# A graph-attention layer and a 64-expert layer in one kernel: the residual of a tile taken one step later, router work inside a tile's products, fewer routing operations on VectorE

## What is computed

```python
xn = layernorm(x);  h = xn @ W.T + b_W
e = (h @ a1)[:, None] + (h @ a2)[None, :] + b_a;  e = where(e > 0, e, 0.2 * e)
x = x + softmax(where(adj > 0, e, -9e15), axis=1) @ h
xf = layernorm(x)
logits = xf @ Wr + br;  topk_logits, topk_idx = top_k(logits, 2);  gates = softmax(topk_logits)
for e in range(64):
    out += combine[:, e:e+1] * (relu(xf @ W1[e] + b1[e]) @ W2[e] + b2[e])
x = x + out
```

## Time and profile before

| what | us |
|---|---|
| median of three runs | 293.51 |
| profiled execution | 295.59 |
| its span, first to last instruction | 293.8 |
| up to the first `scores` | 22.8 |
| attention loop with routing, to the last `place` | 147.2 |
| block tables, padding, first gather | 12.5 |
| 96 expert pairs | 94.5 |
| biases, sums, output | 16.8 |

### The profile page before, as it was taken

The page is one execution under the profiler, slowest core; times in us unless marked ns, Lnnn a source line. Parts: engine busy times, 40 slices in busy tenths (PEclk is TensorE's granted clock), DMA queues, the critical chain, the costliest instruction groups (busy, mean ns, idle before and its releaser), DMA issues.

```text
span 293.8 us, 6191 instructions
## 1 busy us (share of the span) xinstructions
PE 229.1 (78%) x1849; PEld 219.6 (75%) x1849; DVE 220.0 (75%) x643; ACT 173.5 (59%) x386; POOL 167.5 (57%) x193
## 2 busy tenths in 40 slices
PE   1491698596959779586997463999999999999840
PEld 1271698596959769585996352999999999999840
DVE  4858959949599986999997550588888666666554
ACT  2754665755765496567653602688786777777410
POOL 5840104325175982978886565344688888876500
PEclk9998599988897979899799655799999999999995
DMA  6992730644847386150298012212226830100057
GB/s 165 223 190 48 101 62 1 122 130 134 224 74 186 120 214 182 45 232 31 64 425 331 32 48 59 72 58 74 66 81 220 275 138 31 38 27 31 26 186 254
DMA packets 11120, 36.88 MB, mean 126 GB/s; under 512 B 2257, under 2 KB 2833, under 8 KB 10321
## 3 DMA queue, kind: packets, MB, share of 16 engines
q0 software_dynamic: 5232, 14.98, 22.5%
q1 hardware_dynamic: 5424, 21.11, 21.1%
q10 hardware_dynamic: 432, 0.40, 0.6%
HBM read 39.36 MB, written 5.51 MB: 153 GB/s over the span
## 4 chain that ended last, share of the span: by engine, by line
PE 44%; DVE 28%; POOL 9%; DMA 7%; issue 6%; ACT 4%; SPq 1%; POOLq 0%; DVEq 0%; ACTq 0%
PE bank L1089 16%; PE bank L1101 15%; DVE arena L697 7%; PE bank L986 6%; DVE arena L691 6%; POOL rstd L403 3%; POOL table L420 3%; POOL nm L405 2%; DMA arena<-result 2%; DMA xs<-in_x 2%; DVE arena L682 2%; DVE xs L703 1%; PE bank L938 1%; PE bank L1078 1%; ACT rows_in L546 1%
## 5 line engine op out<-in xcount | busy, mean ns | idle before, releaser
L986 PE MATMUL bank<-arena 128*128 128x130 f32 x512 | 64.8, 287 | 3.0 <-ACT arena L540 3.0
L986 PEld LDWEIGHTS bank<-arena 128*128 128x128 f32 x512 | 63.5, 204 | 3.9 <-issue 3.9
L1089 PE MATMUL bank<-arena 128*128 x384 | 61.1, 284 | 0.1
L1101 PE MATMUL bank<-w2s,arena 128*128 x384 | 59.2, 277 | 0.2 <-issue 0.2
L972 PE MATMUL bank<-ident,arena 128*128 128x128 f32 x256 | 39.0, 317 | 22.4 <-DVE arena L697 22.3
L420 POOL DMA_INDIRECT table<-rows_in,pos x32 | 46.8, 1464 | 15.9 <-issue 7.8
L972 PEld LDWEIGHTS bank<-ident,arena 128*128 128x128 f32 x256 | 34.9, 165 | 24.0 <-DVE arena L697 24.0
L1089 PEld LDWEIGHTS bank<-arena 128*128 128x128 f32 x384 | 52.1, 197 | 0.6 <-issue 0.3
L1101 PEld LDWEIGHTS bank<-w2s,arena 128*128 128x128 f32 x384 | 51.1, 194 | 0.6 <-issue 0.6
L868 DVE SCALAR_TENSOR_TENSOR arena<-bank,arena 128x128 f32 x96 | 33.6, 350 | 22.5 <-PE bank L1101 15.2
L599 ACT ACTIVATE arena<-bank,arena 128x128 f32<-128x128 f32 x96 | 35.2, 366 | 19.3 <-PE bank L1089 14.4
(11 more groups left out here) (191 smaller groups left out, 270.9 us busy)
## 6 DMA issues: line engine op xcount, KB each, us to landing
arena<-in_adj POOLq DMA_DIRECT2D x16, 512.0 KB, 6.5
w2s<-in_w SPq DMA_DIRECT2D x8, 768.0 KB
arena<-in_w SPq DMA_DIRECT2D x6, 1024.0 KB
arena<-in_w SPq DMA_DIRECT2D x4, 512.0 KB
w2s<-in_w SPq DMA_DIRECT2D x4, 512.0 KB
xs<-in_x SPq DMA_DIRECT2D x4, 256.0 KB, 6.4
arena<-result SPq DMA_DIRECT2D x2, 512.0 KB, 4.3
arena<-result SPq DMA_DIRECT2D x4, 256.0 KB, 6.2
```

The costliest lines, as they stand in the source:

```text
L986: ins = pe.matmul(OB[t % 2][:, 0:D + 2], pt_r[:, t % 2, j, :], h[:, j, :], start=(j == 0), stop=(j == T - 1))
L1089: ins = pe.matmul(hp(p, b), w1u[:, p % UW, P * b:P * b + P], xT_all[:, bass.ds(column, P)], start=True, stop=True)
L1101: ins = pe.matmul(yp(p), hT[:, p % UH, b, :], w2s[:, bass.ds(u, 1), b, :].rearrange("p e d -> p (e d)"), start=(b == 0), stop=(b == HB - 1))
```

## The change

Four things are altered:

1. **Residual.** VectorE's residual of tile s-3, not s-2, stands in step s, and it stands ahead of leaky(s-1). The statistics of a pair are therefore complete in an even step. GpSimd's `rstd_of` moves to even steps, behind the load of adj; ScalarE's norm(s-4), norm(s-3) stand ahead of evac(s-1) and no longer behind it. The pair 12, 13 is finished behind the loop. Tile 8 is written to the table in step 15, not 14.
2. **Router.** `route_a` and `route_b` of TensorE stand inside attend(LAST + 2): the transposes ahead of its first product, the logits behind the eighth. ScalarE's copy stands between the second and third bank of the same tile's evac.
3. **Fewer operations.** `hot` and `rk` are one operation each over both choices, in place of two. `posf` goes: the position is written as an integer at once. The row numbers (`ids`) are written into `rows_out` once, by GpSimd at the start, and not in each `place`.
4. **Biases.** The last stage's groups are four of four tiles, in place of six.

```diff
     COUNTED = 2
-    INLOOP = 4
-    PLACED = [(0, 0, 8), (0, 1, 9), (0, 2, 10), (0, 3, 11), (1, 4, 12), (1, 5, 13), (1, 6, 13), (1, 7, 14), (2, 8, 14), (2, 9, 15)]
+    PLACED = [(0, 0, 8), (0, 1, 9), (0, 2, 10), (0, 3, 11), (1, 4, 12), (1, 5, 13), (1, 6, 13), (1, 7, 14), (2, 8, 15), (2, 9, 15)]
...
+            pool.tensor_copy(rows_out[:, :, :, ID_COL], ids[:, :, :])
             pool.memset(cnt[:, 0, :], 0.0).then_inc(s_pool, 1)
...
             for s in range(T):
-                if s >= 3 and s % 2 == 1:
-                    rstd_of(s // 2 - 1)
                 if s + 5 < T:
                     load(s + 5)
+                if s >= 4 and s % 2 == 0:
+                    rstd_of(s // 2 - 2)
...
+            rstd_of(6)
             rstd_of(7)
...
             def evac(t):
                 for b in range(4):
+                    for q in range(NG):
+                        if b == 2 and t == LAST[q] + 2:
+                            route_a(q)
...
-                for q in range(INLOOP):
-                    if s == LAST[q] + 3:
-                        route_a(q)
+                if s >= 4 and s % 2 == 0:
+                    norm(s - 4)
+                    norm(s - 3)
                 if s >= 1:
                     evac(s - 1)
-                if s >= 3 and s % 2 == 1:
-                    norm(s - 3)
-                    norm(s - 2)
...
+            norm(T - 4)
+            norm(T - 3)
             evac(T - 1)
             norm(T - 2)
-            route_a(4)
             route_b(4)
...
-                for k in range(TOPK):
-                    ins = dve.tensor_tensor(hot[:, k, kept(q), :],
-                                            iota_e[:, :].rearrange("p (g e) -> p g e", g=1).to_broadcast([P, n, E]),
-                                            idxf[:, rows, k:k + 1].to_broadcast([P, n, E]), ALU.is_equal)
-                link(ins)
+                link(dve.tensor_tensor(hot[:, :, kept(q), :],
+                                       iota_e[:, :].rearrange("p (k g e) -> p k g e", k=1, g=1).to_broadcast([P, TOPK, n, E]),
+                                       idxf[:, rows, :].rearrange("p g (k e) -> p k g e", e=1).to_broadcast([P, TOPK, n, E]), ALU.is_equal))
...
-                link(dve.scalar_tensor_tensor(posf[:, :, 0:n], idxf[:, rows, :].rearrange("p g k -> p k g"), float(STRIDE),
-                                              rank[:, :, 0:n], ALU.mult, ALU.add))
                 dve.wait_ge(s_gate, q + 1)
-                dve.tensor_copy(rows_out[:, rows, :, ID_COL], ids[:, rows, :])
                 dve.tensor_copy(rows_out[:, rows, :, GATE_COL], gate[:, :, rows].rearrange("p k g -> p g k"))
-                dve.tensor_copy(pos[:, rows, :].rearrange("p g k -> p k g"), posf[:, :, 0:n]).then_inc(s_pos, 1)
+                dve.scalar_tensor_tensor(pos[:, rows, :].rearrange("p g k -> p k g"), idxf[:, rows, :].rearrange("p g k -> p k g"), float(STRIDE),
+                                         rank[:, :, 0:n], ALU.mult, ALU.add).then_inc(s_pos, 1)
...
                 if s + 1 < T:
                     penalty(s + 1)
+                if s >= 3:
+                    residual(s - 3)
                 leaky(s - 1)
-                if s >= 2:
-                    residual(s - 2)
...
+            residual(T - 3)
             leaky(T - 1)
             residual(T - 2)
...
             def attend(t):
...
-                if t == T - 1:
-                    route_a(4)
+                for q in range(NG):
+                    if t == LAST[q] + 2:
+                        route_a(q)
                 for j in range(T):
-                    if t == T - 1 and j == T // 2:
-                        route_b(4)
+                    for q in range(NG):
+                        if j == T // 2 and t == LAST[q] + 2:
+                            route_b(q)
```

More of the change, by code:

```diff
@@ L172, in build @@
         rank = sb("rank", [P, TOPK, GRP])
-        posf = sb("posf", [P, TOPK, GRP])
         pos = sb("pos", [P, T, TOPK], I32)
@@ L451, in _ @@
             rstd_of(8)
-            for q in (4, 5):
+            for q in range(4, NG):
                 for t in range(START[q], START[q + 1]):
@@ L622, in _ @@
                     fetch(p + UW - 1)
-            for q in range(NG):
+            for q in range(4):
                 act.wait_ge(s_ct, q + 1)
-                act.activation(combT[:, START[q] * P:START[q + 1] * P], bank[q][:, 0:SIZE[q] * P], ACT.Copy).then_inc(s_cts, 1)
+                act.activation(combT[:, q * 512:q * 512 + 512], bank[q][:, :], ACT.Copy).then_inc(s_cts, 1)
         @block.vector
@@ L899, in _ @@
             dve.tensor_scalar(y_all[:, NB - 1, :], y_all[:, NB - 1, :], slot_gate[:, NB - 1:NB], None, ALU.mult).then_inc(e_last, 1)
-            for q in range(NG):
+            for q in range(4):
                 base(q)
-            dve.wait_ge(s_base, NG)
+            dve.wait_ge(s_base, 4)
             for c in range(2):
@@ L1027, in _ @@
                 attend(s)
-                for q in range(INLOOP):
-                    if s == LAST[q] + 1:
-                        route_a(q)
-                    if s == LAST[q] + 2:
-                        route_b(q)
+                for q in range(NG):
                     if s == LAST[q] + 3:
```

27 lines of the change are left out of this document (13 added, 14 removed).

## The result

The changed kernel takes **281.13 us** (median of 4 runs, 280.18 to 282.84), where the kernel before takes 293.49 (293.38 to 293.85). The ratio is 0.958 with a 95% interval of 0.953 to 0.964: 12.4 us less. The forecast was 8.6 us less, 284.9, with a range from 282.0 to 288.8.

What follows compares the result with a forecast made beforehand. VectorE's list was taken to bound the loop, its waits being what could be gained. The terms -12.3 + 3.8 + 2.1 - 2.2 = -8.6 us from 293.5 gave 284.9 us; eight-in-ten range 282.0 to 288.8.

Steps and rivals of the forecast that it cites:

- The residual wait, -12.3: VectorE's waits at residual's first instruction in the loop: 13.2 us was to become 0.9, so -12.3 us.
- The chain of 11.9 us: From a pair's statistics to the products for residual(3): 14.9 us was to become 11.9, against VectorE's 11.4; wait left 0.5.
- Routing in the loop, +3.8: VectorE's new waits at top2 for logits: 0.7 us each for groups 0 and 1, 2.4 for group 2, 0 for group 3.
- It is 12.9. VectorE has ... 10.5: 2.4 us: Group 2: chain from statistics to logits 12.9 us, with rstd_of queued behind counts(1); VectorE has 10.5 us of work, wait 2.4.
- The end of the loop, +2.1: Group 4's logits: rstd_of 3.5 us late behind six table writes, wait 3.4 us where 1.3 was; bounds 0 and +6.5.
- Fewer operations, -2.2: VectorE's routing operations: 0.37 us saved in each of six groups, -2.2 us; bounds -2.8 and 0.
- the sign of being wrong in the clock: TensorE in the loop: running its odd products in 3.75 us everywhere would show the forecast wrong about the clock.
- A: Rival: all waits go, no new ones come, GpSimd's pair slips in, writes short: 278.1 us, between case near 282; chance 0.10.
- B: Rival: routing waits take more, through lower clock at two more groups and slow writes: 289 to 290 us; with D 0.14.
- C: Rival: slower, evac of the odd tile behind the norms, its wait reaching VectorE whole at seven places: 304 us; chance 0.04.
- D: Rival: GpSimd's table writes set the end, half of the gain goes: 289 us; chance 0.14 together with B.
- The rule weighed: Skill's inference that leaky leaves descriptor writes alone, so a table write costs 1.0 us; forecast kept the longer 2.48 us.

Runs made afterwards that it cites:

- Experiment 4's third kernel: Changed kernel with tile 9's table writes behind rstd_of(6), top2(3) behind the last leaky, and top2(0), top2(1) one step later: 281.46 us, ratio 0.959.
- experiment 4's first kernel: Changed kernel with the table writes of tile 9 moved behind rstd_of(6) on GpSimd's list: 281.13 us, ratio 0.954.
- experiment 1: Changed kernel with the old routing operations: 283.73 us, ratio 0.966; kernel before with only the fewer operations: 291.23 us, ratio 0.989.
- experiment 2: Changed kernel with residual(s-2) behind leaky(s-1): 298.6 us, ratio 1.016; with rstd_of also back in odd steps: 286.56 us, ratio 0.972.
- the third set: Kernels run on one chip beside the kernel before (293.46 us); the changed kernel, run again unaltered, took 280.13 us there, ratio 0.957.
- experiment 5: Changed kernel with six bias groups: 281.84 us, ratio 0.959; with twelve idle transposes behind products of tiles 6, 10, 12: 279.89 us, ratio 0.956.

## Why the prediction was wrong

Its direction and its mechanism held: the residual wait went, the logits' waits came in its place, and the operations gave a little. Terms of its sum were mis-sized, and most of them in one direction.

*The residual wait, -12.3: right, the last tenths by chance.* It measured 0.9 us where 0.9 was forecast, by 0.61 for the first tile (0.4) and none at residual(3) (0.5), and 0.27 at a place that the count had not named. The chain of 11.9 us measured 10.1, nearly all of the difference because it kept products of 5.5 us, which took 3.82.

*Routing in the loop, +3.8: the step that failed.* "The wait is 0.7, for groups 0 and 1 each" measured 0.79 and 0.79. "It is 12.9. VectorE has ... 10.5: 2.4 us" for group 2 measured 0: 2.4 us of the miss. The chain there took 8.2 us to the end of the logits. Of its 12.9, "3.9 us late" measured 3.1, the "3.1, near the middle" of GpSimd's pair 1.0, norms and hand-over 1.0 for 1.2, and the "1.7 for products at the lower clock" nothing. On GpSimd:

```profile
104.49 2.28 POOL L411 TENSOR_TENSOR cnt_t<-cnt,both 128x64 bf16<-128x64 bf16 x1 [3.48 <-DVE both L735]
106.85 1.01 POOL L411 TENSOR_TENSOR cnt_t<-cnt_t,both 128x64 bf16<-128x64 bf16 x2
107.94 0.31 POOL L413 TENSOR_TENSOR cnt<-cnt_t,both 128x64 bf16<-128x64 bf16 x1
108.40 0.99 POOL L419 DMA_INDIRECT table<-rows_in,pos  x1 [0.15 <-issue]
109.69 2.07 POOL L419 DMA_INDIRECT table<-rows_in,pos  x1 [0.30 <-issue]
111.78 0.73 POOL L402 TENSOR_TENSOR rstd<-ve,expo 128x2 f32<-128x2 f32 x1
112.59 0.19 POOL L404 TENSOR_TENSOR nm<-nm,rstd 128x2 f32<-128x2 f32 x1
```

The statistics were ready at 108.67, so `rstd_of` was 3.1 us late and not 3.9: the two counting operations at 106.85 take 1.01 us, where they took 2.94 before under a leaky. The write that leaky held ends 0.8 us behind leaky (begun at 108.59, 2.34 us long), and the pair of operations behind it falls into VectorE's small instructions of place(1), the first and last of which are:

```profile
110.85 0.16 DVE L742 TENSOR_SCALAR gs<-ge 128x4 f32<-128x4 f32 x1
...
112.85 0.16 DVE L753 SCALAR_TENSOR_TENSOR pos<-idxf,rank 128x8 int32<-128x8 f32 x1
```

"It starts at no fixed place of VectorE's step" was the error: the forecast itself had place(1), 1.9 us without a wide operation, on VectorE's list right behind leaky. The last 1.7 us, the lower clock, was not paid either (TensorE):

```profile
110.98 1.97 PE L968 MATMUL bank<-ident,arena 128*128 128x128 f32 x16 [2.47 <-DVE arena L697]
...
114.44 2.06 PE L984 MATMUL bank<-arena 128*128 128x130 f32 x16
116.34 0.55 PE L1000 MATMUL bank<-wts,x2T 128*128 128x64 f32 x4
```

The logits end at 116.89 and VectorE arrives at 118.99, with 2.1 us in hand. Experiment 4's third kernel shows the other side. There the statistics are taken up 4.8 us late, the pair takes 2.8 us and the clock falls, and the chain is 13.8 us against VectorE's 10.6: a wait of 3.24. So the three terms are real; in the changed kernel none came at its full size.

*The end of the loop, +2.1: right at one place, wrong at the next.* Group 4 waits 2.87 us where 3.4 was forecast (`rstd_of` was 3.1 us late, not 3.5: statistics at 138.04, `rstd_of` at 141.16). Group 5's wait was left as it was, at 1.04 us, and is 2.39, the second step that failed. The order there is as before: residual(15), place(4), top2(5). But VectorE has place(4) done 1.5 us after the statistics (151.36), where it took 2.5 (163.33); of the 1.0 us between them 0.5 is the fewer operations and 0.5 a wait at `rk` that is gone. And the chain to the end of the logits takes 3.9 us where it took 3.5, since TensorE's last part is longer (before, then after):

```profile
163.45 0.89 PE L1002 MATMUL bank<-wts,x2T 128*128 128x64 f32 x4 [0.47 <-ACT x2T L553]
```

```profile
152.60 1.11 PE L1000 MATMUL bank<-wts,x2T 128*128 128x64 f32 x4 [0.47 <-ACT x2T L555]
```

So the time that place(4) saves is waited for at once in top2(5). The two waits together are 5.3 us where 4.4 was forecast. They also vary from one execution to the next: the changed kernel's three traces have 2.87 and 2.39, 1.57 and 2.40, 3.20 and 1.69.

*The wait for `rk`: not in the sum.* It fell from 1.8 to 0.7 us, and why is not shown. Before, both waits end after the counting products have ended in the trace, by 1.65 us for group 4 (160.20 and 161.85) and 0.64 for group 5; after, the one wait ends with the products (157.16 and 157.20). The waits of 2.3 us in experiment 4's first kernel are of the first kind.

*Fewer operations, -2.2.* The list gave 3.1 (2.4 and 2.5 by experiment 1). The rows of one group after:

```profile
80.03 0.68 DVE L747 TENSOR_TENSOR rk<-bank,hot 128x512 f32<-128x512 f32 x1
80.75 0.69 DVE L750 TENSOR_REDUCE rank<-rk 128x8 f32<-128x512 f32 x1
81.47 0.17 DVE L752 COPY rows_in<-gate 128x8 f32<-128x8 f32 x1
81.55 0.16 DVE L753 SCALAR_TENSOR_TENSOR pos<-idxf,rank 128x8 int32<-128x8 f32 x1
81.62 2.28 DVE L691 CUSTOM_DVE_ANT_0 arena<-arena 128x2048 f32<-128x2048 bf16 x1
```

From `rk` to the next scores it is 1.59 us; before it was 1.93 from 89.67 to 91.60: 0.34 there and 0.07 in `hot`, so 0.41 a group for 0.37. Six of them are 2.5. The rest of the 3.1, 0.6 us, I have no row for. By experiment 1 one us on the list is worth about half a us of time in the changed kernel, so this term does not simply add up with the waits.

Against the forecast then: group 2 -2.4, `rk` -1.1, operations -0.9, group 4 -0.5, group 5 +1.4, groups 0 and 1 +0.2, and the stages outside the loop -0.6 (no term had them). That is -3.9, and the difference to explain is -4.1 (12.7 between the two spans, 8.6 forecast).

*The signs.* Two of the forecast's own signs went against it. TensorE ran the products of every odd tile at the higher clock (3.75 to 3.82 us whole, 1.95 to 2.06 a half), which was the sign of being wrong in the clock; the lower clock fell on transposes instead (79.68 and 127.65), behind which nothing waited in this trace. And VectorE's stage is 135.1 us, not 138 to 139. The reciprocal's wait, the logits' waits in the loop (1.6 us in all, under the 7 named) and the stage of pairs came as said.

*The rivals.* A has the nearest number, the case near 282 us, but it came by another way. Its reason, that GpSimd's pair slips in unheld, holds at 111.78 and 141.16 and not in step 4 (48.30), and its short writes did not come: the six between the statistics of tiles 10, 11 and those of 12, 13 took 0.96 to 2.94 us. B's extra clock losses stayed away from the waits in this trace; in the changed kernel's second one group 3's logits wait 0.40 us behind transposes of 3.67. C did not come in the changed kernel, where residual has the third step, but experiment 2 went over to the slower side by one step: 296 us, through GpSimd's queue, with 8.24 of 15.5 us in one place. D's writes did not set the end: GpSimd stood idle 2.10 us ahead of those of group 5.

*The rule weighed.* A write that begins under leaky takes long in the trace after as well:

```profile
116.75 2.32 DVE L697 SCALAR_TENSOR_TENSOR arena<-arena,tneg 128x2048 f32<-128x2048 f32 x1
```

```profile
116.42 0.96 POOL L419 DMA_INDIRECT table<-rows_in,pos  x1 [0.31 <-issue]
117.69 2.22 POOL L419 DMA_INDIRECT table<-rows_in,pos  x1 [0.30 <-issue]
```

The write begun at 117.69 under this leaky ends 0.84 us after it; the one begun at 116.42, 0.33 us ahead of leaky, took 0.96. But a load of adj, which GpSimd also issues, takes its usual time when it begins under leaky (VectorE, then GpSimd):

```profile
85.45 2.32 DVE L697 SCALAR_TENSOR_TENSOR arena<-arena,tneg 128x2048 f32<-128x2048 f32 x1
```

```profile
86.17 0.62 POOL L370 DMA_DIRECT2D arena<-in_adj  x1
```

Two more begin under a leaky, at 30.32 and 35.39, and take 0.53 us; those with nothing wide beside them take 0.53 to 0.62 in the two traces. The Trainium skill, "SBUF — State Buffer", section "Who interferes with whom", infers that such a VectorE operation leaves descriptor writes alone. The loads agree, and the prediction's "the trace disagrees" goes further than its rows: the transfers that are held are those that have positions to read (`table<-rows_in,pos`). Whether that reading is what is held no run here separates. For the sum nothing changes, since the table writes are of the held kind.

*What the experiments leave open.* In the third set the changed kernel's six runs lie at 279.7 to 280.4 us (four) and at 282.3 and 282.4 (two). Its traced spans, 281.1 us at the result and 278.1 in the third set, differ by about as much. They part at the start, where TensorE runs four transposes and eight products in 1.06 and 1.93 us (14.71, 15.57) in the one and in 0.71 and 1.06 in the other (14.83, 15.38), so that VectorE's first scores come at 23.2 and at 21.9, and by stretches at the lower clock in the loop (below). What decides it stays open; filling three gaps (experiment 5) did not change it. So the 4.1 us explained above are those of one pair of traces, and the trace of 278.1 us would ask for 3.0 more.

## What to carry to other kernels

When a wait is removed, follow the released engine to the next thing that it needs: here 12.3 us went and 4.4 came back at the logits, and without their place in the middle of a product 6 to 7 more would have. An instruction on a queue that runs in order is as late as all that stands ahead of it there: moving one consumer by one step turned a hidden queue into a wait of 8.2 us. Don't take the middle of a held and an unheld duration: look at what the other engine's list holds at that time. GpSimd's pair took 1.0 us beside place(1) (111.78) and 4.4 beside leaky and scores (48.30), in the same kernel.

## What the runs showed of the hardware that was not expected

The same idle gap on TensorE did not always cost the clock. In two traces of the changed kernel, with the same instructions and the same gap (first the one with a span of 281.1 us, then the one of 278.1):

```profile
79.68 3.39 PE L968 MATMUL bank<-ident,arena 128*128 128x128 f32 x16 [2.40 <-DVE arena L697]
```

```profile
77.70 1.97 PE L968 MATMUL bank<-ident,arena 128*128 128x128 f32 x16 [2.40 <-DVE arena L697]
```

Sixteen transposes take 3.39 us in the one, most of it at the lower of the two levels (1.2 GHz; granted clock 0.56), and 1.97 in the other, at the higher (2.4 GHz; 1.00). In the kernel's three traces the gap of 2.4 us cost the clock once, the one of 2.47 us (110.98, above) never, and one of 2.83 us twice. A forecast for one such place can only give both values.
